# Loading a convolution kernel's input in whole units, issued behind the preceding unit's stores

## The chip, the cores and the metric

The kernel runs on one core of one Trainium2 chip. The metric is the device time of one execution in microseconds (us); lower is better. The core has a matrix engine (PE), a vector engine (DVE), a scalar engine (ACT), a general engine (POOL), and a sync engine (SP) that here does nothing but issue DMA transfers. The transfers run on 16 DMA engines.

## What is computed

`x` is float32 of shape (32, 384, 56, 56). Each image's 384 channels fall into 32 groups of 12. Each group is normalised by its own mean and variance, then each channel is convolved along the height, circularly, with its own 56 taps, a bias is added, and `x` is added back:

```python
x_cat = jnp.concatenate([x, x[:, :, :-1, :]], axis=2)
out = jax.lax.conv_general_dilated(x_cat, weight, window_strides=(1, 1), padding='VALID', dimension_numbers=('NCHW', 'OIHW', 'NCHW'), feature_group_count=x.shape[1])
...
m = jnp.mean(g, axis=(2, 3, 4), keepdims=True)
s = jnp.var(g, axis=(2, 3, 4), keepdims=True)
...
x = x + _L0_conv_ref(_gn(x), L0_conv_weight, L0_conv_bias)
```

## The kernel before, in words

The work is cut into 64 **units** (`UNITS`). A unit is one channel group of 16 images, laid out as 112 partitions (2 images' 56 rows each) by 5376 float32 values, and is kept as two **halves** of 2688 values: half 0 holds channels 0 to 5, half 1 channels 6 to 11. In DRAM the input is padded to 128 partitions, so a half is 1344 KB to load and 1176 KB to store. `xt` has six slots (`XS = 6`), each for one unit; unit n uses slot n % 6. The result is written over the input in the same slot and stored from there, so a slot takes its next load only after its stores have landed. Two units share a set of filter matrices `runs`, which come from `taps` in two transfers of 147 KB each (`load_taps`).

What each engine does for a unit:

- **DVE** runs three units ahead with the statistics: 16 `bn_stats` for unit u + 3 (`stats`, eight on each half) stand between the six evictions of the even channels of unit u (`take`). Before its first instruction on half 0 it waits for that half's load, and before its ninth for half 1. The order in a unit is: 3 chunks, take channel 0, 3 chunks, take 2, 2 chunks, take 4, `add_vars`, 3 chunks (the first of half 1), take 6, `invert`, 2 chunks, take 8, 3 chunks, take 10.
- **POOL** makes small sums of the statistics and the Newton steps for unit u + 2, and adds `x` to the odd channels of unit u (`add_x`), three before the Newton steps and three behind them.
- **ACT** normalises unit u + 1 into `xn` and evicts the odd channels of unit u.
- **PE** does 12 convolutions (`convolve`) for a unit and small matmuls for unit u + 2.

**SP** issues every transfer, in one fixed order and on one queue; an instruction that waits holds all behind it. A half can be stored once DVE's and POOL's last channel of it is done (`store`). For unit u the order is: store half 0 of u; load half 1 of unit u + 5; store half 1 of u; on every odd u the taps of a later group; load half 0 of unit u + 6. Each load waits for the landing of the same half's store from its slot: half 1 of unit u - 1, half 0 of unit u. All six slots are loaded at the start, twelve half loads, with taps and bias between them.

I write S(u,h) for the store and L(n,h) for the load of a half, and L(n) for the load of a whole unit.

Of the kernel before, what the change touches and what calls it, by code (L numbers as in the profile page):

```python
# [13 lines left out]
GROUPS = 32  # L14
# [9 lines left out]
HALVES = 2  # L24
# [5 lines left out]
PER_GROUP = UNITS // GROUPS  # L30
# [6 lines left out]
XS = 6  # L37
# [11 lines left out]
def through(channels, u, c):  # L49

    return u * len(channels) + sum(k <= c for k in channels)


def build(nc, x, taps, bias, out):
    with ExitStack() as ctx:
        def sb(name, shape):
            return ctx.enter_context(nc.sbuf_tensor(name, shape, F32))
# [4 lines left out]
        def sem(name):  # L62
            return ctx.enter_context(nc.semaphore(name))

        xt = sb("xt", [ROWS, XS, HALVES, FREE])
# [23 lines left out]
        p_mean = psum("p_mean", [P, 512])  # L89
        p_var = psum("p_var", [P, 512])  # L90

        x_loaded = [[sem(f"x_loaded{s}_{h}") for h in range(HALVES)] for s in range(XS)]
        out_stored = [[sem(f"out_stored{s}_{h}") for h in range(HALVES)] for s in range(XS)]
        taps_loaded = [sem(f"taps_loaded{s}") for s in range(2)]
        bias_loaded = sem("bias_loaded")
# [19 lines left out]
        def channel_of(tile, slot, c):  # L115
            half = tile[0:P, slot, c // CH, :].rearrange("k (b c w) -> k b c w", b=BP, c=CH)
            return half[:, :, c % CH, :]

        def bias_of(u, c):
            k = u // PER_GROUP * CG + c  # L120
            return bias_all[:, k:k + 1]
# [4 lines left out]
        def bank_bw(c):  # L126
            return bank(c).rearrange("k (b w) -> k b w", b=BP)
# [2 lines left out]

        @block.sync
        def _(sp):
            def load(n, h):
                if n >= UNITS:
                    return
                if n >= XS:
                    sp.wait_ge(out_stored[n % XS][h], 16 * (n // XS))
                sp.dma_start(xt[:, n % XS, h, :], x[n, :, h, :]).then_inc(x_loaded[n % XS][h], 16)

            def load_taps(g):  # L140

                for par in range(PAR):
                    sp.dma_start(runs[par * H:(par + 1) * H, g % 2, par * BLOCK:(par + 1) * BLOCK], taps[g]
                                 ).then_inc(taps_loaded[g % 2], 16)

            def store(u, h):
                last = (h + 1) * CH - 1
                sp.wait_ge(dve_taken, through(DVE_CH, u, last))
                sp.wait_ge(pool_added, through(ACT_CH, u, last))
                sp.dma_start(out[u, :, h, :], xt[0:P, u % XS, h, :]).then_inc(out_stored[u % XS][h], 16)  # L150

            for h in range(HALVES):
                load(0, h)
            for h in range(HALVES):
                load(1, h)
            sp.wait_ge(runs_zeroed, 1)
            load_taps(0)
            sp.dma_start(bias_all[:], bias.broadcast_to([P, C])).then_inc(bias_loaded, 16)
            for n in range(2, XS):
                for h in range(HALVES):  # L160
                    load(n, h)
                if n == 3:
                    load_taps(1)

            for u in range(UNITS):
                store(u, 0)
                if u >= 1:
                    load(u - 1 + XS, 1)
                store(u, 1)
                g = u // PER_GROUP + 2  # L170
                if u % PER_GROUP == PER_GROUP - 1 and g < GROUPS:
                    load_taps(g)
                load(u + XS, 0)
            for s in range(XS):
                for h in range(HALVES):
                    sp.wait_ge(out_stored[s][h], 16 * len(range(s, UNITS, XS)))
# [77 lines left out]
        @block.vector  # L254
        def _(dve):
            nc.vector.memset(eps[:], EPS).then_inc(consts_set, 1)
            nc.vector.memset(runs[:], 0.0).then_inc(runs_zeroed, 1)

            def stats(n, k0, k1):
                for k in range(k0, k1):  # L260
                    h, b = k // BP, k % BP
                    if b == 0:
                        dve.wait_ge(x_loaded[n % XS][h], 16 * (n // XS) + 16)
                    ins = nc.vector.bn_stats(st[:, n % RS, h, b, :], xt[0:P, n % XS, h, b * ROW:(b + 1) * ROW])  # L264
                if k1 == HALVES * BP:
                    ins.then_inc(stats_ready, 1)

            def add_vars(n):
                dve.wait_ge(pvar_ready, n + 1)
                parts = p_var[:, n % RS * SUBS:(n % RS + 1) * SUBS]  # L270
                nc.vector.tensor_reduce(var[:, n % RS, :], parts.rearrange("k (h b e) -> k b h e", h=HALVES, b=BP),  # L271
                                        AXIS.XY, ALU.add).then_inc(var_ready, 1)

            def invert(n):
                dve.wait_ge(std_ready, n + 1)
                nc.vector.reciprocal(r0[:, n % RS, :], std[:, n % RS, :]).then_inc(r0_ready, 1)  # L276

            def take(u, c):
                dve.wait_ge(conv_ready, u * CG + c + 1)
                cell = channel_of(xt, u % XS, c)  # L280
                nc.vector.scalar_tensor_tensor(out=cell, in0=bank_bw(c), scalar=bias_of(u, c), in1=cell,  # L281
                                               op0=ALU.add, op1=ALU.add).then_inc(dve_taken, 1)

            ALL = HALVES * BP
            stats(0, 0, ALL)
            stats(1, 0, ALL // 2)
            add_vars(0)
            stats(1, ALL // 2, ALL * 3 // 4)
            invert(0)
            stats(1, ALL * 3 // 4, ALL)  # L290
            stats(2, 0, ALL // 2)
            add_vars(1)
            stats(2, ALL // 2, ALL * 3 // 4)
            invert(1)
            stats(2, ALL * 3 // 4, ALL)

            dve.wait_ge(bias_loaded, 16)
            ends = (3, 6, 8, 11, 13, 16)
            for u in range(UNITS):
                for k, c in enumerate(DVE_CH):  # L300
                    if u + LEAD_STATS < UNITS:
                        stats(u + LEAD_STATS, ends[k - 1] if k else 0, ends[k])
                    take(u, c)
                    if u + LEAD_COEF < UNITS:
                        if k == 2:
                            add_vars(u + LEAD_COEF)
                        if k == 3:
                            invert(u + LEAD_COEF)
# [138 lines left out]
```

## Time and profile before

| | |
|---|---|
| median of 3 runs (shown) | 880.48 us |
| the profiled execution, its time | 881.76 us |
| its span, first to last instruction | 879.9 us |
| busy: PE, DVE, ACT, POOL | 83%, 77%, 75%, 65% of the span |
| chain that ended last | DMA 52%, PE 13%, POOL 13%, ACT 10%, DVE 8% |
| moved by DMA | 340.64 MB, mean 387 GB/s |
| read and written in DRAM | 185.97 MB, 154.14 MB |
| TensorE clock granted, mean | 0.925 |

The page divides the span into 40 equal slices and gives each engine's busy share in tenths. DMA's row gives the mean over 16 DMA engines. The chain is followed back from the last instruction to whatever released each step. A transfer's time to landing runs from its issue on SP until its last byte is in place, time in the queue behind other transfers included.

### The profile page before, as it was taken

To read this page: it belongs to the slowest core of one execution; us is meant where nothing else is said; L and a number is where in the kernel's file an instruction comes from. 1 tells how busy PE (TensorE), PEld (TensorE's weight loads), DVE (VectorE), ACT (ScalarE), POOL (GpSimd) and SP (SyncE) were. 2 spreads that over 40 slices of the span, in tenths; PEclk is the share of its full clock that TensorE was granted. 3 is DMA by queue.
4 is the path that set the end of the run, shared out by engine and by line. 5 is a ranking of instruction groups with operands and counts; after the bars stand their busy time and mean duration, and the time that the engine had idled before them with its cause. 6 is when DMAs were issued, how large, how long until landed. Compare 5 with 4: busy or idle time off the path is not lost.

```text
span 879.9 us, 8182 instructions
## 1 busy us (share of the span) xinstructions
PE 732.7 (83%) x1920; PEld 513.0 (58%) x1920; DVE 679.5 (77%) x1538; ACT 662.8 (75%) x1026; POOL 571.2 (65%) x1102
## 2 busy tenths in 40 slices
PE   0688898889889888878788887988878988889895
PEld 0456666666566666556565564665655656566664
DVE  7888878897787878778777677877877887788842
ACT  1788788788788878778677776787877867778784
POOL 2467767676676666666675656676766667567665
PEclk9999979998898999899898899899989989899998
DMA  9999999999999999999999999999999999999986
GB/s 355 410 387 399 383 407 396 406 413 410 403 394 374 377 391 389 405 392 388 401 381 396 370 361 386 398 403 398 403 389 387 392 402 400 390 401 409 405 306 229
DMA packets 39472, 340.64 MB, mean 387 GB/s; under 512 B 5008, under 2 KB 5120, under 8 KB 8704
## 3 DMA queue, kind: packets, MB, share of 16 engines
q1 hardware_dynamic: 39424, 340.13, 99.1%
q8 instruction: 15, 0.25, 0.1%
q14 instruction: 33, 0.27, 0.1%
HBM read 185.97 MB, written 154.14 MB: 387 GB/s over the span
## 4 chain that ended last, share of the span: by engine, by line
DMA 52%; PE 13%; POOL 13%; ACT 10%; DVE 8%; issue 3%; SPq 0%; POOLq 0%; ACTq 0%
DMA out<-xt 28%; DMA xt<-x 24%; PE conv L402 12%; POOL xt L235 10%; ACT xn L330 7%; DVE st L264 5%; ACT xn L338 3%; DVE xt L281 2%; PE p_mean L378 1%; POOL newt L227 1%; POOL rstd L228 1%; POOL newt L226 1%; POOL newt L225 1%; POOL shift L229 0%; PE p_var L387 0%
## 5 line engine op out<-in xcount | busy, mean ns | idle before, releaser
L402 PE MATMUL conv<-xn,runs 112*112 112x448 f32 x1536 | 694.5, 602 | 24.6 <-DMA runs<-taps 10.9
L330 ACT ACTIVATE xn<-xt,shift,rstd 112x672 f32<-112x672 f32 x512 | 463.1, 942 | 140.1 <-POOL xt L235 140.1
L402 PEld LDWEIGHTS conv<-xn,runs 112*112 112x112 f32 x1536 | 465.6, 314 | 167.3 <-issue 64.7
L264 DVE BATCH_NORM_STATS2 st<-xt 112x6 f32<-112x336 f32 x1024 | 451.4, 494 | 109.5 <-DMA xt<-x 109.3
L235 POOL TENSOR_TENSOR xt<-xt,xn 112x448 f32<-112x448 f32 x384 | 431.2, 1136 | 81.0 <-ACT xn L338 80.8
L281 DVE SCALAR_TENSOR_TENSOR xt<-conv,bias_all,xt 112x448 f32<-112x448 f32 x384 | 258.5, 673 | 81.1 <-PE conv L402 80.5
L338 ACT ACTIVATE xn<-conv,bias_all 112x448 f32<-112x448 f32 x384 | 235.7, 626 | 47.7 <-PE conv L402 44.9
L378 PE MATMUL p_mean<-msum,neg_mean 112*112 112x8 f32 x128 | 24.5, 263 | 112.2 <-POOL msum L204 112.2
L214 POOL TENSOR_TENSOR dev<-st,nmean 112x16 f32<-112x16 f32 x128 | 24.9, 216 | 134.6 <-ACT nmean L314 134.6
L378 PEld LDWEIGHTS p_mean<-msum,neg_mean 112*112 112x112 f32 x128 | 19.3, 191 | 150.2 <-POOL msum L204 134.4
L386 PEld LDWEIGHTS p_var<-st,avg 112*112 112x112 f32 x128 | 23.6, 210 | 40.6 <-POOL dev L218 25.9
L225 POOL TENSOR_TENSOR newt<-r 112x8 f32<-112x8 f32 x64 | 12.8, 200 | 35.1 <-DVE r L276 32.6
L386 PE MATMUL p_var<-st,avg 112*112 112x32 f32 x128 | 24.9, 281 | 2.1 <-POOL dev L218 2.1
L387 PE MATMUL p_var<-dev,avg_dev 112*112 112x32 f32 x128 | 26.0, 288 | 0.0
L201 POOL TENSOR_TENSOR mpart<-st 112x16 f32<-112x16 f32 x64 | 15.1, 235 | 10.8 <-DVE st L264 10.8
L319 ACT ACTIVATE std<-var,eps 112x8 f32<-112x8 f32 x64 | 18.9, 295 | 4.2 <-DVE var L271 4.2
L314 ACT COPY nmean<-p_mean 112x8 f32<-112x8 f32 x64 | 9.5, 149 | 15.6 <-PE p_mean L378 15.6
L387 PEld LDWEIGHTS p_var<-dev,avg_dev 112*112 112x112 f32 x128 | 20.9, 208 | 0.0
L223 POOL TENSOR_SCALAR hv<-var 112x8 f32<-112x8 f32 x64 | 12.7, 198 | 9.7 <-DVE var L271 4.4
L218 POOL TENSOR_TENSOR dev<-dev 112x32 f32<-112x32 f32 x64 | 15.4, 240 | 5.0
L227 POOL TENSOR_TENSOR newt<-newt,three_halves 112x8 f32<-112x8 f32 x64 | 13.2, 206 | 5.0
L228 POOL TENSOR_TENSOR rstd<-newt,r 112x8 f32<-112x8 f32 x64 | 13.0, 203 | 5.0
(23 smaller groups left out, 69.4 us busy)
## 6 DMA issues: line engine op xcount, KB each, us to landing
xt<-x SPq DMA_DIRECT2D x128, 1344.0 KB, 10.6
out<-xt SPq DMA_DIRECT2D x128, 1176.0 KB, 12.9
runs<-taps SPq DMA_DIRECT2D x64, 147.0 KB
bias_all<-bias SPq DMA_DIRECT2D x1, 168.0 KB, 14.1
```

The costliest lines, as they stand in the source:

```text
L214: ins = nc.gpsimd.tensor_tensor(d[:, h], means, nm, ALU.add)
L227: chained(nc.gpsimd.tensor_tensor(newt[:], newt[:], three_halves[:], ALU.add))
L228: chained(nc.gpsimd.tensor_tensor(rstd[:, r, :], newt[:], r0[:, r, :], ALU.mult))
L235: nc.gpsimd.tensor_tensor(cell, cell, channel_of(xn, u % NS, c), ALU.add).then_inc(pool_added, 1)
L264: ins = nc.vector.bn_stats(st[:, n % RS, h, b, :], xt[0:P, n % XS, h, b * ROW:(b + 1) * ROW])
L281: nc.vector.scalar_tensor_tensor(out=cell, in0=bank_bw(c), scalar=bias_of(u, c), in1=cell, op0=ALU.add, op1=ALU.add).then_inc(dve_taken, 1)
L330: ins = nc.scalar.activation(xn[:, n % NS, :, part], xt[0:P, n % XS, :, part], ACT.Identity, scale=rstd[:, n % RS, b:b + 1], bias=shift[:, ...
L338: nc.scalar.activation(channel_of(xn, u % NS, c), bank_bw(c), ACT.Identity, bias=bias_of(u, c)).then_inc(act_evicted, 1)
L378: nc.tensor.matmul(p_mean[:, n % RS * BP:(n % RS + 1) * BP], neg_mean[:], msum[:, n % RS, :], start=True, stop=True).then_inc(mean_ready, 1)
L386: nc.tensor.matmul(dst, avg[:], squares, start=True, stop=False)
L387: nc.tensor.matmul(dst, avg_dev[:], dev[:, r, :], start=False, stop=True).then_inc(pvar_ready, 1)
L402: nc.tensor.matmul(bank(c), lay[:, :, c], channel_of(xn, u % NS, c), start=True, stop=True).then_inc(conv_ready, 1)
```

## The change

A unit is loaded in one transfer of 128 x 5376 values, with one semaphore per slot. The load waits for both stores from its slot. For unit u SP's order is now: S(u,0), S(u,1), the taps on odd u, L(u + 5), whose slot is that of unit u - 1. DVE waits for a whole unit ahead of its first `bn_stats`. Stores are halves as before, and what the compute engines execute is the same.

```diff
-            def load(n, h):
+            def load(n):
                 if n >= UNITS:
                     return
                 if n >= XS:
-                    sp.wait_ge(out_stored[n % XS][h], 16 * (n // XS))
-                sp.dma_start(xt[:, n % XS, h, :], x[n, :, h, :]).then_inc(x_loaded[n % XS][h], 16)
+                    for h in range(HALVES):
+                        sp.wait_ge(out_stored[n % XS][h], 16 * (n // XS))
+                sp.dma_start(xt[:, n % XS, :, :], x[n]).then_inc(x_loaded[n % XS], 16)
...
             for u in range(UNITS):
-                store(u, 0)
+                for h in range(HALVES):
+                    store(u, h)
+                    g = u // PER_GROUP + 2
+                    if h == 1 and u % PER_GROUP == PER_GROUP - 1 and g < GROUPS:
+                        load_taps(g)
+
                 if u >= 1:
-                    load(u - 1 + XS, 1)
-                store(u, 1)
-                g = u // PER_GROUP + 2
-                if u % PER_GROUP == PER_GROUP - 1 and g < GROUPS:
-                    load_taps(g)
-                load(u + XS, 0)
+                    load(u - 1 + XS)
...
-                    if b == 0:
-                        dve.wait_ge(x_loaded[n % XS][h], 16 * (n // XS) + 16)
+                    if k == 0:
+                        dve.wait_ge(x_loaded[n % XS], 16 * (n // XS) + 16)
```

SP's queue of before, at the first stores of the run (units 0 and 1), with the semaphores that each row waits for; `out_stored0_1` counts stores of half 1 from slot 0:

```order
L150 DMA out<-xt 112x2688 [waits pool_added,dve_taken] x2
L138 DMA xt<-x 128x2688 [waits out_stored0_0]
L150 DMA out<-xt 112x2688 [waits pool_added,dve_taken]
L138 DMA xt<-x 128x2688 [waits out_stored0_1]
L150 DMA out<-xt 112x2688 [waits pool_added,dve_taken]
L143 DMA runs<-taps 56x672 x2
L138 DMA xt<-x 128x2688 [waits out_stored1_0]
```

The same place of the changed kernel, followed by unit 2:

```order
L151 DMA out<-xt 112x2688 [waits pool_added,dve_taken] x4
L144 DMA runs<-taps 56x672 x2
L139 DMA xt<-x 128x5376 [waits out_stored0_1,out_stored0_0]
L151 DMA out<-xt 112x2688 [waits pool_added,dve_taken] x2
L139 DMA xt<-x 128x5376 [waits out_stored1_1,out_stored1_0]
```

Before, L(6,0) stands behind two stores and L(6,1) behind three. Now L(6) stands behind four stores and the taps. Later in the queue every load used to stand between two stores; now two stores stand between two loads.

## Rows read from the trace of the kernel before

**Rows 1.** The page: engines' busy time, and DMA's busy tenths in 40 slices.

```profile
PE 732.7 (83%) x1920; PEld 513.0 (58%) x1920; DVE 679.5 (77%) x1538; ACT 662.8 (75%) x1026; POOL 571.2 (65%) x1102
...
DMA  9999999999999999999999999999999999999986
```

**Rows 2.** Stretches: length, busy of PE, PEld, DVE, ACT, POOL, clock, DMA share, GB/s.

```profile
5.00:12.00 7.00, 0.00 (x0) 0.00 (x0) 5.33 (x13) 0.00 (x0) 0.00 (x0) 1.00 1.01 429
...
300.00:830.00 530.00, 450.31 (x1176) 312.95 (x1176) 412.84 (x941) 403.81 (x626) 348.69 (x667) 0.92 1.01 393
866.00:873.00 7.00, 5.61 (x15) 4.15 (x14) 2.74 (x4) 2.81 (x5) 5.24 (x6) 1.00 0.92 307
```

**Rows 3.** Waits of SP's queue, whole run: total us, times, longest.

```profile
SPq L138 <- DMA out<-xt: 518.0, 115, 7.3
```

**Rows 4.** Waits, 300 to 830 us.

```profile
DVE st L264 <- DMA xt<-x: 103.7, 72, 3.3
```

**Rows 5.** Waits, 90 to 290 us.

```profile
DVE xt L281 <- PE conv L402: 35.6, 36, 2.1
...
DVE st L264 <- DMA xt<-x: 0.2, 1, 0.2
```

**Rows 6.** Chain that ended last, in time: start, us, what; first and last of 15 units.

```profile
91.90 3.27 POOL xt L235 x3
...
271.99 3.27 POOL xt L235 x3
```

**Rows 7.** The same chain later: start, us, what.

```profile
376.93 13.26 DMA out<-xt
390.20 10.29 DMA xt<-x
400.51 1.33 DVE st L264 x3
```

**Rows 8.** The load's line L138, 300 to 830 us: issue to landing.

```profile
DMA to landing us min/median/max: 9.5/10.6/12.3
```

**Rows 9.** The store's line L150, 300 to 830 us: issue to landing.

```profile
DMA to landing us min/median/max: 11.7/13.0/17.3
```

**Rows 10.** Timeline of unit 29: start, us, engine, line, operation [idle before <- releaser].

```profile
407.73 1.33 DVE L264 BATCH_NORM_STATS2 st<-xt 112x6 f32<-112x336 f32 x3 [1.99 <-DMA xt<-x]
...
412.79 0.18 DVE L271 TENSOR_REDUCE var<-p_var 112x8 f32<-112x32 f32 x1
...
414.57 1.33 DVE L264 BATCH_NORM_STATS2 st<-xt 112x6 f32<-112x336 f32 x3 [1.60 <-DMA xt<-x]
...
418.03 3.31 POOL L235 TENSOR_TENSOR xt<-xt,xn 112x448 f32<-112x448 f32 x3
```

**Rows 11.** DVE's timeline at the start: the wait for half 0 of unit 2.

```profile
21.95 3.38 DVE L264 BATCH_NORM_STATS2 st<-xt 112x6 f32<-112x336 f32 x8 [1.72 <-DMA xt<-x]
```

**Rows 12.** SP's timeline, 52 to 59 us: S(1,0), L(6,1), S(1,1), taps.

```profile
52.62 0.32 SPq L150 DMA_DIRECT2D out<-xt  x1
52.99 0.42 SPq L138 DMA_DIRECT2D xt<-x  x1
57.60 0.32 SPq L150 DMA_DIRECT2D out<-xt  x1
57.97 1.08 SPq L143 DMA_DIRECT2D runs<-taps  x2
```

**Rows 13.** Landing of L(6,0) (least) and L(6,1) (most), issued from 49.57 us.

```profile
DMA to landing us min/median/max: 7.8/9.5/11.2
```

**Rows 14.** Landing of the run's first four half loads; the first finds an empty queue.

```profile
DMA to landing us min/median/max: 5.8/10.0/14.4
```

**Rows 15.** DVE's timeline at the end: the last unit's two halves arrive.

```profile
828.11 1.33 DVE L264 BATCH_NORM_STATS2 st<-xt 112x6 f32<-112x336 f32 x3 [1.52 <-DMA xt<-x]
...
834.15 1.33 DVE L264 BATCH_NORM_STATS2 st<-xt 112x6 f32<-112x336 f32 x3 [0.80 <-DMA xt<-x]
```

More of the change, by code:

```diff
@@ L90, in build @@
         p_var = psum("p_var", [P, 512])
-        x_loaded = [[sem(f"x_loaded{s}_{h}") for h in range(HALVES)] for s in range(XS)]
+        x_loaded = [sem(f"x_loaded{s}") for s in range(XS)]
         out_stored = [[sem(f"out_stored{s}_{h}") for h in range(HALVES)] for s in range(XS)]
@@ L150, in store @@
                 sp.dma_start(out[u, :, h, :], xt[0:P, u % XS, h, :]).then_inc(out_stored[u % XS][h], 16)
[L152 to L155, printed above, removed]
+            load(0)
+            load(1)
             sp.wait_ge(runs_zeroed, 1)
@@ L159, in _ @@
             for n in range(2, XS):
-                for h in range(HALVES):
-                    load(n, h)
+                load(n)
                 if n == 3:
```

## The prediction

> **What bounds the kernel now.** I read the page first. PE is the busiest engine at 83%, DVE follows at 77%, but the DMA row stands at 9 from the first slice to the thirty-eighth [rows 1]. By stretches the 16 DMA engines are fully busy (share 1.01) from 300 to 830 us, where they move 393 GB/s [rows 2]. So over most of the run there is no gap that a better order of transfers could fill.
>
> The waits say who follows whom. From 90 to 290 us DVE hardly waits for loads (0.2 us) and waits for PE instead [rows 5]; the chain passes through POOL, ACT and PE, and the fifteen POOL steps from 91.90 to 271.99 us are 14 units apart, 12.86 us a unit [rows 6]. From 300 us on DVE waits 103.7 us in 72 pieces for loads [rows 4]. The chain there is a store's landing (13.26 us), then a load's (10.29 us), then DVE [rows 7]. A unit moves 2 x 1344 + 2 x 1176 + 147 KB = 5.31 MB, which at 393 GB/s is 13.5 us. This is what was measured: L(6,1) was issued at 52.99 and landed 11.2 us later, at 64.2 [rows 12, 13]; L(63,1), the last load, released DVE at 834.15 [rows 15]; the 57 units between took 770 us, 13.51 us each. The six units loaded at the start let compute run at its own 12.86 us for 290 us, and then the supply of data sets the pace.
>
> By the bytes, a half load is 3.5 us of queue, a half store 3.06 us, the taps 0.38 us a unit. The landing times agree: a load has load, store, load to drain (10.1 us; median 10.6 [rows 8]), and a store load, store, load, store (13.1 us; median 13.0 [rows 9]). So a landing time in the middle is queue, with about 0.5 us on top. On an empty queue it is otherwise: the first load took 5.8 us [rows 14], of which its bytes at 429 GB/s [rows 2] are 3.2, so 2.6 us is start and finish.
>
> **The change part by part.**
>
> *SP's wait.* SP sat 518.0 us waiting for stores to land before it could issue loads [rows 3]. In the new order the load waits for stores of the unit before, the later of which was issued a unit (13.5 us) ago and has only what was queued plus 3.1 us ahead. Nearly all of the 518 us goes. It is worth nothing by itself: while SP waited the DMA engines were busy (1.01). Stores now leave when they are computed instead of up to a unit later, and the queue gets shorter by that.
>
> *Does the shorter queue run dry?* One lap spans two units: S(u,1) is issued, L(u+5) behind it lands, DVE starts unit u+2 with it, and S(u+2,1) becomes ready. From DVE's start at 407.73 to the end of POOL's last add at 421.34 is 13.6 us, less the 1.60 us wait at mid-unit [rows 10], 12.0 us. The transfer part is 3.06 + 0.38 + 7.0 + 0.5 = 10.9 us. The lap is 22.9 us plus whatever is still queued when S(u,1) is issued. Two units of DMA work are 27.0 us, so 4.1 us remain queued, more than the 2.6 us of an empty queue's start. On average it stays fed, by 1.5 us. Cost taken 0, and the other end is a rival.
>
> *The start: the first cost.* DVE waited until 21.95 us for half 0 of unit 2 [rows 11]. It now waits for the whole unit, one half load later, 3.2 us at 429 GB/s [rows 2]. `add_vars(1)` stands behind these statistics, ACT's `root(1)` behind that, and the first convolutions behind ACT, so all evictions slip by about 3.3 us. S(1,1) was issued at 57.60 us when compute released it, and is now ready at 60.9. L(6), two half loads that went out at 49.57 and 52.99 us, waits behind it and behind the taps' issue of 1.08 us [rows 12]. All initial loads and S(0,0), S(0,1) have drained by then, so the queue is dry before S(1,0) and again before S(1,1). S(1,1) lands at 60.9 + 2.6 + 3.0 = 66.5 us, and taps and L(6) at 66.5 + 0.4 + 7.0 = 74 us. Before, L(6,1) landed at 64.2. The queue is ten microseconds behind, and since it is the bound from there on, nothing makes them good. The cover that used to exist, the six preloaded units, is spent on this.
>
> *The middle.* 57 units of 13.51 us from 74 us put the landing of L(63) at 844 us, if bytes move as fast as now.
>
> *The end: the second cost.* Before, the last arrival is half 1 of unit 63, at 834.15 us, in the middle of unit 60; half 0 was there at 828.11 [rows 15]. From there to the end of the span are 879.9 - 834.15 = 45.75 us. Now DVE cannot begin unit 60 until the whole unit is in. The part of DVE's unit ahead of half 1 is from 828.11 to 834.15 - 0.80 = 5.2 us, the same as from 407.73 to 412.97 in unit 29 [rows 10]. The tail becomes 51.0 us.
>
> *Sum so far.* 844.1 + 51.0 = 895.1 us of span, 15.2 us more than 879.9.
>
> *Two stores in a row.* The nearest rows for traffic of one kind: loads alone ran at 429 GB/s; in the last stores' stretch, 307 GB/s at a share of 0.92, that is 334 GB/s [rows 2]. Wholly separated, a unit would take 2.41 MB / 334 = 7.2 us for stores and 2.75 / 429 = 6.4 for loads, 14.0 with taps, 0.5 us more than mixed, 28 us in 57 units. The other end: blocks twice as long make no difference, or a long load sheds part of the gap between 393 and 429 GB/s. A block is 6 to 7 us and transfers overlap at its borders, so I take a quarter, +7 us, nearer the mixed row because it is this queue's own.
>
> Span 902 us; the execution's time lies 1.86 us over its span, and the median shown is 1.3 us under the profiled time: 903 us.
>
> A rule that speaks for the change: the Trainium skill (DMA: Bandwidth & Descriptors, "Anatomy of one DMA" and "Bandwidth") gives a transfer from the GpSimd path about 2.0 us fixed plus its bytes at 436 GB/s and advises batches of 1 MiB or more. If each of the 63 merges saved that fixed part, an estimate by that page is 126 us less transfer time. The rows with a full queue, a landing time equal to the sum of the bytes ahead plus 0.5 us, show the fixed part covered by its neighbours.
>
> **The rivals.**
>
> 1. *Same costs at start and end, but the mixed rate holds or improves slightly.* For: loads alone are faster, and a whole load has one start instead of two. Against: the 334 GB/s of stores alone. 895 + 0.6 = 896 us; with 1% less per unit, 888.
> 2. *The queue runs dry in the middle.* The 1.5 us margin is a mean; a slow unit of compute (intervals between POOL's steps reach over 13 us where the clock drops) uses 1 us of it, and the 16 engines need not be in step, so some go idle first. The deciding point is less than 2.6 us queued at S(u,1). At 0.3 to 0.5 us lost a unit on top of the forecast: 920 to 931 us.
> 3. *Faster.* Long loads run at the pure-load rate without stores suffering, until compute's 12.86 us [rows 6] sets the pace: 74 + 57 x 12.86 + 51.0 = 858 us. It needs 0.65 us less per unit, that is 413 GB/s in place of 393 with 44% of the bytes stores. The break-even with 880.5 is 13.25 us a unit. The skill's rule above would act here, and the result would be this, since compute then stops it.
>
> **How the numbers follow.** The forecast (897 to 912 us) gets 0.40, rival 1 (888 to 897) 0.25, rival 2 (over 912) 0.22, rival 3 (under 863) 0.06, and 0.07 lies between 863 and 888. Within 2% of 880.5, about what a measurement tells from no change, ends at 898. So slower 0.60, same 0.34, faster 0.06. The range is 885 to 926: it takes in rival 1 and most of rival 2, and leaves out the full 28 us of separated traffic with a dry queue on top.
>
> **What would show it.** SP's wait for stores nearly gone from its waits. DVE's first wait for unit 2 ending near 25.2 us; L(6) issued near 62 us and landed near 74; DMA below full in the second slice's end and the third (44 to 66 us), about 8 us lost. Then full until about 840. DVE's waits at one place in a unit, not two. A span from L(63)'s arrival to the end of 51 us. GB/s from 300 to 830 of 385 to 393 by the forecast; over 400 would mean rival 3, and a DMA share below 0.97 there rival 2. Wrong at the root would be an L(6) that lands before 68 us, or a tail near 46.

## The result

| | before | changed |
|---|---|---|
| median | 881.64 us (4 runs) | 956.27 us (4 runs, 953.01 to 964.67) |
| ratio | | 1.0909, 95% interval 1.0852 to 1.0966 |
| profiled execution, its time | 881.76 us | 953.01 us |
| its span | 879.9 us | 951.3 us |
| mean DMA rate over the span | 387 GB/s | 358 GB/s |

The change costs 9%. Slower was forecast, at 903 us with a range up to 926; the measured loss is over three times the forecast one, and the range missed it.

Some runs of a kernel come out more than 1.5% above its fastest, and one of the four runs before took 1353.82 us; such runs are left out of the ratios, and of the times given for the experiments below. The two medians of the table alone would give 1.085 in place of the recorded 1.0909, which changes nothing in what follows. An experiment's ratio is to the kernel before, run beside it on the same chip, and experiments are compared with one another by these ratios, since the kernel before itself came out between 873 and 881 us from one set of runs to the next.

### The profile page after: what moved, and what is told of

The parts are those of the page before. It is cut to its first block, busy times and chain, and to the rows that moved or that the text cites. A ratio compares the mean times of both kernels' runs of the same rounds, so it can differ in the third digit from the quotient of the medians.

```text
span 951.3 us, 8176 instructions
## 1 busy us (share of the span) xinstructions
PE 754.4 (79%) x1920; PEld 511.5 (54%) x1920; DVE 669.1 (70%) x1538; ACT 667.6 (70%) x1026; POOL 569.2 (60%) x1102
## 4 chain that ended last, share of the span: by engine, by line
DMA 47%; DVE 22%; POOL 15%; PE 6%; SPq 4%; ACT 2%; issue 2%; POOLq 0%; ACTq 0%
DMA xt<-x 47%; DVE st L262 14%; POOL xt L233 11%; DVE xt L279 7%; PE conv L400 6%; SPq L144 3%; ACT xn L328 2%; SPq L151 1%; ACT xn L336 1%; POOL newt L225 1%; POOL rstd L226 1%; POOL newt L224 1%; POOL newt L223 1%; POOL shift L227 1%; DVE r L274 0%
## 5 line engine op out<-in xcount | busy, mean ns | idle before, releaser
L400 PE MATMUL conv<-xn,runs 112*112 112x448 f32 x1536 | 718.8, 616 | 57.7 <-ACT xn L328 49.0
L400 PEld LDWEIGHTS conv<-xn,runs 112*112 112x112 f32 x1536 | 463.6, 315 | 223.3 <-ACT xn L328 78.1
L199 POOL TENSOR_TENSOR mpart<-st 112x16 f32<-112x16 f32 x64 | 15.0, 234 | 14.7 <-DVE st L262 14.7
## 6 DMA issues: line engine op xcount, KB each, us to landing
xt<-x SPq DMA_DIRECT2D x64, 2688.0 KB, 15.2
```

The costliest lines, as they stand in the source:

```text
L400: nc.tensor.matmul(bank(c), lay[:, :, c], channel_of(xn, u % NS, c), start=True, stop=True).then_inc(conv_ready, 1)
```

## The profile after

The page of the changed kernel, with engines' busy time, DMA's busy tenths and rate in 40 slices, and the transfers (count, KB each, median us to landing):

```profile
PE 754.4 (79%) x1920; PEld 511.5 (54%) x1920; DVE 669.1 (70%) x1538; ACT 667.6 (70%) x1026; POOL 569.2 (60%) x1102
...
DMA  9979999999999999999999999999999999999956
GB/s 363 396 254 377 377 373 383 378 356 363 363 371 364 360 360 377 369 359 365 381 368 372 372 374 375 363 372 371 369 347 370 364 379 378 365 376 363 346 184 223
...
xt<-x SPq DMA_DIRECT2D x64, 2688.0 KB, 15.2
out<-xt SPq DMA_DIRECT2D x128, 1176.0 KB, 9.9
```

Against [rows 1] the DMA row has a dent in the third slice (254 GB/s), at the place where L(6) is late. After that it reads 9 as before, yet the rate is some 370 GB/s where it was 393 [rows 2]. A busy share in tenths hides this. From 100 to 800 us (the five engines, then clock, DMA share, GB/s):

```profile
100.00:800.00 700.00, 574.03 (x1452) 385.08 (x1452) 501.62 (x1160) 504.39 (x778) 430.02 (x825) 0.91 0.98 369
```

What engines waited for, in the whole run (total us, times, longest), first DVE's waits, then SP's:

```profile
DVE st L262 <- DMA xt<-x: 239.2, 62, 6.8
```

```profile
SPq L150 <- POOL xt L233: 680.6, 127, 36.3
SPq L151 <- DVE xt L279: 22.8, 27, 2.3
```

SP's 518 us for stores to land [rows 3] are gone, as forecast. DVE now waits for a load once in a unit, not twice, but 239 us in all, where it was 109 us before. SP waits for POOL, that is for stores to be ready: it is no longer ahead of compute.

The start and the end, in SP's timeline and in DVE's timeline of the changed kernel:

```profile
61.37 0.32 SPq L151 DMA_DIRECT2D out<-xt  x1
61.73 1.67 SPq L144 DMA_DIRECT2D runs<-taps  x2
63.50 2.06 SPq L139 DMA_DIRECT2D xt<-x  x1
```

```profile
25.91 3.38 DVE L262 BATCH_NORM_STATS2 st<-xt 112x6 f32<-112x336 f32 x8 [0.97 <-DMA xt<-x]
...
898.33 1.33 DVE L262 BATCH_NORM_STATS2 st<-xt 112x6 f32<-112x336 f32 x3 [2.88 <-DMA xt<-x]
```

L(6) was issued at 63.50 and released DVE at 76.64; L(63), the last load, released it at 898.33. So the span splits as the forecast did:

| part | before | forecast | changed |
|---|---|---|---|
| arrival of the first refill, L(6,1) or L(6) | 64.2 us | 74 us | 76.6 us |
| 57 units | 13.51 us each | 13.51 + 0.12 us | 14.42 us each |
| from the last arrival to the end | 45.75 us | 51.0 us | 53.0 us |

Start and end cost 12.4 and 7.2 us, the middle 57 x 0.91 = 51.9 us. They make up the 71.4 us between the spans. The middle is what the forecast missed.

The chain of the changed kernel, in time (start, us, what), over one lap of two units:

```profile
88.62 0.32 SPq L151
88.99 1.41 SPq L144
90.44 2.03 SPq L144
92.57 14.36 DMA xt<-x
106.96 1.33 DVE st L262 x3
...
115.60 3.27 POOL xt L233 x3
118.94 0.32 SPq L151
119.30 0.41 SPq L144
119.76 1.24 SPq L144
121.10 12.78 DMA xt<-x
133.90 1.33 DVE st L262 x3
```

L(8) is issued at 92.57 and lands 14.4 us later; DVE to POOL's last add takes 11.9 us; then SP issues the store and the taps, and L(10) at 121.10. This lap returns to the end of the run. Its mean is 2 x 14.42 = 28.8 us. Over the laps from unit 3 to unit 56 that is 12.1 of compute (median 12.0), 2.0 from the last store's issue to the load's, and 14.7 for the load's landing. On odd units, with the taps' issue in between, the last two are 3.5 and 13.3 us, on even units 0.4 and 16.2: nearly the same sum.

A load lands when the last of the 16 engines has done its share. Counted from the landings' records between 100 and 800 us, the first engine is done 11.6 us after the load's issue and the last 14.9 us (medians); the typical distance between them is 3.2 us. By then the engines that were done first have run out of work. Stretches of 2 us around and behind the issue of a load at 525.54 us (columns as above):

```profile
524.00:526.00 2.00, 2.00 (x6) 0.90 (x4) 2.00 (x6) 2.00 (x4) 1.65 (x4) 0.50 0.99 370
526.00:528.00 2.00, 2.00 (x5) 1.20 (x6) 2.00 (x6) 0.91 (x2) 1.14 (x1) 0.50 1.01 296
528.00:530.00 2.00, 2.00 (x4) 0.99 (x3) 1.60 (x6) 1.75 (x4) 1.04 (x1) 0.50 0.96 335
```

The rate falls to 296 GB/s and the share stays at 1.01. The share counts a packet, that is one row's transfer, in the stretch in which it starts, so in stretches this short it can't show a gap. The packets' own records do: from 526 to 528 us 13 of the 16 engines are at work on average. Between 100 and 800 us it is 15.6 of 16, before 15.9; in the two microseconds from 1 us after a load's issue it is 14.7. The gaps belong to the odd units, which have the taps ahead of their load: at the issue of S(u,1) of an odd u 13.6 engines are at work and five to seven microseconds later 13.5, while around S(u,1) of an even u it is never under 15.8.

The packets also take longer. A load's row of 21,504 bytes takes 932 ns on average and a store's row of 10,752 bytes 446 ns, together 457 ns for each 10,752 bytes; before, the rows of loads and stores together took 438 ns. So 1.9% of the lost rate is idle engines and 4.3% is longer packets: about 0.3 and 0.6 us a unit.

## The experiments

Two theories were set against each other. The **lap theory**: a unit's load goes out too late, and the lap shown above holds the pace. The **traffic theory**: two stores in a row, or rows of 21,504 bytes, are slower traffic whatever waits for them. Below, L139 and so on are the load's line in each kernel, and a window row has the DMA share and GB/s last. 5.31 MB divided by that rate is the time of a unit.

**Half loads in the changed order.** The edit is against the kernel before.

```diff
             for u in range(UNITS):
                 store(u, 0)
-                if u >= 1:
-                    load(u - 1 + XS, 1)
                 store(u, 1)
...
-                load(u + XS, 0)
+                if u >= 1:
+                    for h in range(HALVES):
+                        load(u - 1 + XS, h)
```

> The changed order kept (S(u,0), S(u,1), taps, then the load of unit u + 5), but the load goes out as two half loads with a semaphore each, as in the kernel before. Two theories of the changed kernel's 14.4 us a unit. Lap theory: the load is issued too late, and a two-unit lap of landing 14.4 us, compute 12.0 us and issue time sets the pace; half 0 lands some 3.5 us before the whole unit did, so DVE starts earlier, the lap shrinks by up to 3.5 us, and the pace goes back to about 13.5 us a unit: 885 to 900 us. Traffic theory: two stores in a row and loads in blocks twice as long move slower on the 16 engines, whatever is waited for; the blocks are the same here, so 940 to 956 us. If only the 21,504-byte rows are slow: about 905 us with DVE's waits for the first half still there.

911.64 us, ratio 1.0449 (1.0375 to 1.0523). The window from 100 to 800 us:

```profile
100.00:800.00 700.00, 591.33 (x1518) 405.39 (x1517) 528.17 (x1218) 527.16 (x811) 451.89 (x863) 0.91 1.00 385
```

13.8 us a unit, against 14.4. By the ratios the new order alone costs 4.5% and the merge another 4.6%, about 40 us each. The result lies outside what either theory gave, above the lap theory's range, and nearest to the third guess, that the rows of 21,504 bytes alone are slow. That guess is answered in the main by the packets: with seven slots, below, such a row takes 880 ns, twice a half load's row here (444 ns). In the same order a half load changes that row length and when DVE may start.

**The whole load behind the first store.**

```diff
             for u in range(UNITS):
-                for h in range(HALVES):
-                    store(u, h)
-                    g = u // PER_GROUP + 2
-                    if h == 1 and u % PER_GROUP == PER_GROUP - 1 and g < GROUPS:
-                        load_taps(g)
-
+                store(u, 0)
                 if u >= 1:
                     load(u - 1 + XS)
+                store(u, 1)
+                g = u // PER_GROUP + 2
+                if u % PER_GROUP == PER_GROUP - 1 and g < GROUPS:
+                    load_taps(g)
```

> Whole loads, but L(u + 5) is issued behind S(u,0) and ahead of S(u,1), half a unit (about 7 us) earlier. The blocks of one kind in the queue are as long as in the changed kernel: one whole load, then two half stores. Lap theory: the lap loses up to 7 us and DMA alone sets the pace: 13.5 to 13.7 us a unit, 890 to 905 us. Traffic theory: the pace stays at 14.2 to 14.4 us, 940 to 955 us.

978.32 us, ratio 1.1218 (1.1101 to 1.1334): slower than the changed kernel, which neither theory said. The window, what SP waited for and how long a store took to land, from 100 to 800 us:

```profile
100.00:800.00 700.00, 562.63 (x1401) 370.53 (x1401) 481.40 (x1115) 484.28 (x745) 413.90 (x792) 0.91 0.95 353
```

```profile
SPq L138 <- DMA out<-xt: 564.5, 47, 13.7
```

```profile
DMA to landing us min/median/max: 11.9/15.2/17.6
```

Earlier in the order is not earlier in time. L(u+5) waits for S(u-1,1), which was issued just behind L(u+4). Stores land 15.2 us after their issue, those of half 1 14.5 to 14.9 us. That makes a lap of one unit, with at most S(u,0) in the queue when it closes. 5.31 MB at 353 GB/s are 15.0 us, near that landing. My expectation had left out what the moved load waits for.

**The taps behind the load.**

```diff
             for u in range(UNITS):
-                for h in range(HALVES):
-                    store(u, h)
-                    g = u // PER_GROUP + 2
-                    if h == 1 and u % PER_GROUP == PER_GROUP - 1 and g < GROUPS:
-                        load_taps(g)
-
+                store(u, 0)
+                store(u, 1)
                 if u >= 1:
                     load(u - 1 + XS)
+                g = u // PER_GROUP + 2
+                if u % PER_GROUP == PER_GROUP - 1 and g < GROUPS:
+                    load_taps(g)
```

> The changed kernel with the taps issued behind the whole load instead of ahead of it. Lap theory: the taps' two issues on SP took 1.7 to 3.5 us on every second unit ahead of the load; off the lap, 1 to 1.7 us a unit less can be had until DMA binds: 880 to 930 us, likeliest 910. Traffic theory: same bytes, same blocks, 950 to 956 us.

942.1 us, ratio 1.0787 (1.0694 to 1.0879). That is 11 to 14 us less than the changed kernel, under the 26 to 76 us that I expected, and its interval overlaps the changed kernel's, so the gain itself is not clear. The loads' median landing rose from 15.2 to 16.0 us while the issue time ahead of them went down. So most of the 1.7 to 3.5 us that SP spent on the taps was not a delay by itself; time taken from the issue comes back in the queue, as in the odd and even laps of the changed kernel above.

**Seven slots.** `XS = 7` in the changed kernel and in the kernel before.

> The changed kernel with seven slots for units instead of six; everything is waited for one unit earlier relative to its use, so a lap spans three units (39 us for two units' worth of slack before). Lap theory: the lap no longer binds, DMA does, at 13.5 to 13.7 us a unit, and seven preloaded units soften the start: 880 to 900 us. Traffic theory: pace 14.2 us or more: 935 to 950 us.

> The kernel before with seven slots. DMA sets its pace already, so lead is worth nothing in the middle: 13.5 us a unit, 872 to 885 us. Control for the changed kernel with seven slots: if seven slots gave 30 us or more here too, that run would say nothing of the change's lap.

The changed kernel takes 900.93 us, ratio 1.0317 (1.0205 to 1.0429). The kernel before takes 877.7 us, ratio 1.0019 (0.9964 to 1.0073). The changed kernel with seven slots, its window and its transfers:

```profile
100.00:800.00 700.00, 595.97 (x1539) 409.34 (x1538) 530.71 (x1223) 532.94 (x821) 454.10 (x874) 0.91 1.00 388
```

```profile
xt<-x SPq DMA_DIRECT2D x64, 2688.0 KB, 20.9
out<-xt SPq DMA_DIRECT2D x128, 1176.0 KB, 21.8
```

By this rate the changed kernel's unit takes 13.7 us; from the landing of L(7) to that of L(63) it is 13.87 us. By the ratios 5.9%, 52 us, of the loss are gone, with order, blocks and row length unchanged. Of the 46 us between the two profiled spans, 31 lie in the middle. 13 lie at the start, where the seventh preloaded unit covers the late first refill (L(7) lands at 77.9 us in place of 90.9), and 2 at the end. The same slot is worth nothing to the kernel before. Transfers now take 21 us to land and it does no harm, though the first and the last engine of a load are 11 us apart: the queue is deep. This is the strongest evidence for lead. A load's row of 21,504 bytes takes 880 ns here, so most of the slower packets are not a matter of their length either.

**Lead taken from the kernel before.** `XS = 5`, order and half loads as before.

> The kernel before with five slots: a unit of lead is taken from it, order and half loads stay. Lap theory: S(u-1,1) to the landing of L(u+4,1) to S(u+1,1) is 6.8 + 10.6 + 6.8 us = 24.2 us plus backlog, close to the 22.9 us of the changed kernel, so it should run at 14.0 to 14.6 us a unit: 908 to 942 us. If the changed kernel's extra time is not a matter of lead but of whole loads, 880 to 890 us.

913.17 us, ratio 1.0423 (1.0332 to 1.0514), at the near end of the lap theory's range. The window and what SP waited for, from 100 to 800 us:

```profile
100.00:800.00 700.00, 603.42 (x1529) 411.71 (x1528) 537.50 (x1221) 529.17 (x816) 452.00 (x865) 0.89 1.00 386
```

```profile
SPq L149 <- POOL xt L235: 421.6, 101, 7.0
SPq L138 <- DMA out<-xt: 136.9, 81, 4.8
```

SP waits for compute here, as in the changed kernel; with six slots its wait for POOL in this stretch was 4.3 us. But only the time fell into the range. The pace is 13.75 us a unit and not the 14.0 to 14.6 of the lap theory. Of the 31 us between the spans 14 lie at the start (L(6,1) lands at 78.1 us in place of 64.2), 14 in the middle and 3 at the end. Lead matters to this kernel without any merged load, by 0.24 us a unit in the middle.

**Both cures.** The changed order with half loads and seven slots.

> The changed order with half loads and seven slots. The lap is then as long as can be: what is left over the kernel before is the order's cost in traffic plus the late first store-to-load step. By the traffic runs alone 0.2 to 0.35 us a unit: 885 to 900 us. If half loads and seven slots cure different things, the gain over the seven-slot run with whole loads is more than 10 us.

889.5 us, ratio 1.011 (1.0059 to 1.0161), from six of its ten runs; the others took 900 to 922 us. With whole loads and seven slots the ratio was 1.0317 (1.0205 to 1.0429), so half loads still gain 2.1%, 18 us, over it. That is more than the 10 us by which my expectation would tell two cures of different things. Separately half loads win back 4.6% and the slot 5.9%, together 8.0%: they cure in part the same thing and in part not. About the same 1.7% lies between whole and half loads in the transfers alone, below, so the part that lead does not cure may be traffic. That is not shown.

**The transfers alone.** Three kernels contain only SP's part: every transfer of the full kernel, and stores that wait for their own load in place of compute. No statistics, convolution or addition is done. The taps wait in addition for the landing of the set before them in the same place. The edit of the store for the transfers as before:

```diff
-                sp.wait_ge(dve_taken, through(DVE_CH, u, last))
-                sp.wait_ge(pool_added, through(ACT_CH, u, last))
+                sp.wait_ge(x_loaded[u % XS][h], 16 * (u // XS) + 16)
```

> SP's queue of the kernel before alone: the same transfers in the same order, all compute left out, so the output is the padded input's first 112 rows; a store waits only for its own load, a load for its slot's store. The queue is never short of work. Both theories: the pace of the full kernel was DMA's, so 64 units of 13.4 us, less the tail: 850 to 865 us. If compute's own memory traffic slows the DMA engines, it is nearer 800 us (430 GB/s).

> The changed kernel's transfers in their order (whole loads of 21,504-byte rows, two half stores in a row), all compute left out. Traffic theory: blocks of one kind and long rows are slow in themselves: 3 to 5% over the traffic of the kernel before alone, 880 to 905 us. Lap theory: nothing is late here, so within 1.5% of it, the active work of a unit measured with seven slots being 1% over that of before.

> The transfers of the run with half loads in the changed order, all compute left out: tells long rows from long blocks. If blocks cost and rows do not, equal to the changed traffic; if rows cost, equal to the traffic of before; by the lap theory all three are within 1.5%.

> The traffic of the kernel before alone, once more, beside the two changed forms on one chip: 865 to 872 us.

> The changed kernel's traffic alone, again: 891 us as before, 2 to 3% over the traffic of before.

> Half loads in the changed order, alone; the first time 875 and 903 us left it open. If the cost of the changed traffic lies in blocks of one kind, 889 to 893 us, the same as with whole loads; if in the long rows, 865 to 872 us.

| transfers alone | first | again | ratio to the full kernel before, again |
|---|---|---|---|
| as before | 866.8 us | 865.9 us | 0.9881 (0.9758 to 1.0004) |
| as changed | 891.4 us | 890.4 us | 1.0154 (1.003 to 1.0277) |
| changed order, half loads | 875.5 us (the other run 903) | 876.7 us (three runs; the other seven 886 to 917) | 0.9982 (0.9899 to 1.0064) |

The first row shows that the kernel before is bound by its transfers: without any compute they take within 1.5% of its time, a little more than the 850 to 865 us expected. From 100 to 800 us they moved, first as before and then as changed,

```profile
100.00:800.00 700.00, 0.00 (x0) 1.00 1.01 395
```

```profile
100.00:800.00 700.00, 0.00 (x0) 1.00 1.00 389
```

The full kernel before moved 393, so compute hardly slows them. The second row is the traffic theory's part: 24 us over 64 units, 0.37 us a unit, and that with a full queue. Between the landings of L(6) and L(63) in the profiled runs it is 0.31 us a unit (13.42 and 13.73). These 2.8% lie between what the two theories gave, 3 to 5% and under 1.5%. The third row lies between and spreads too far; whether long blocks or long rows cost these 24 us stays open.

**A thin queue without compute.** The changed transfers alone, a unit's stores held until the load four units on has landed.

```diff
-                last = (h + 1) * CH - 1
-                sp.wait_ge(dve_taken, through(DVE_CH, u, last))
-                sp.wait_ge(pool_added, through(ACT_CH, u, last))
+                m = min(u + 4, UNITS - 1)
+                sp.wait_ge(x_loaded[m % XS], 16 * (m // XS) + 16)
```

> The changed kernel's transfers alone, with the stores of unit u held until the load of unit u + 4 has landed, so that the queue runs dry once a unit. If an almost empty queue by itself makes the load's packets slow (932 ns for 21,504 bytes in the changed kernel, 1011 behind the first store, 878 with a full queue), they are over 930 ns here too and a unit takes more than 13.66 + 2.6 = 16.3 us. If it was compute's presence, packets stay near 880 ns and a unit takes about 16 us.

1141.44 us in a single run, 18.1 us a unit:

```profile
100.00:800.00 700.00, 0.00 (x0) 1.00 0.82 294
```

The load's rows took 858 ns, not over 930, and the store's rows 540 ns. The loads' part of this expectation fell: a queue that runs dry does not by itself make the loads' rows slow. But it does make rows slow. Loads and stores together took 481 ns for 10,752 bytes, where the same transfers with a full queue took 439 ns, and no compute ran in either. And compute's presence alone is not the cause, since with seven slots the loads' rows are at 880 ns beside full compute. So longer packets go with a thin queue, in the changed kernel as here. Why, and why once the loads' rows and once the stores', is open.

**Padding and rows.** Two runs on what limits the kernel before. Loads of 112 rows in place of 128:

```diff
-                sp.dma_start(xt[:, n % XS, h, :], x[n, :, h, :]).then_inc(x_loaded[n % XS][h], 16)
+                sp.dma_start(xt[0:P, n % XS, h, :], x[n, 0:P, h, :]).then_inc(x_loaded[n % XS][h], 16)
```

> The kernel before, loading only the 112 rows that are used and not the 16 rows of padding: an eighth of the load bytes less, 4.96 MB a unit in place of 5.31. If bytes on the DMA engines are what bounds the kernel before, a unit takes 12.6 us of DMA, compute's 12.86 us takes over, and the time is about 64 + 57 x 12.86 + 46 = 843 us, 840 to 855. If 7 rows per engine move slower than 8 (the stores' stretch at the end ran at 334 GB/s), the gain is lost: 875 us or more.

926.02 us, ratio 1.0544 (1.0469 to 1.0619), with 7% fewer bytes. And stores of 128 rows in place of 112, the padding dropped on the host:

```diff
-                sp.dma_start(out[u, :, h, :], xt[0:P, u % XS, h, :]).then_inc(out_stored[u % XS][h], 16)
+                sp.dma_start(out[u, :, h, :], xt[:, u % XS, h, :]).then_inc(out_stored[u % XS][h], 16)
```

> The kernel before with stores of 128 rows (the 16 rows of padding written too, and dropped on the host): 2.75 MB a unit stored in place of 2.41. Loads of 112 rows moved at 356 GB/s overall where loads of 128 gave 393, with packets of 482 ns in place of 437. If transfers of 112 rows are slow because of how rows fall to the engines, all packets come near 404 ns: 5.65 MB at up to 430 GB/s, 13.15 to 13.5 us a unit, 862 to 880 us. If bytes alone count, 5.65 MB at 393 GB/s is 14.4 us a unit: 930 us or more.

889.98 us, ratio 1.0103 (1.0048 to 1.0157), with 6% more bytes; this is outside both ranges, nearer to the first. Windows of the two, loads of 112 rows first:

```profile
100.00:800.00 700.00, 584.42 (x1503) 400.99 (x1504) 526.63 (x1201) 519.68 (x802) 443.49 (x853) 0.91 1.01 356
```

```profile
100.00:800.00 700.00, 594.91 (x1563) 411.85 (x1563) 548.19 (x1249) 538.83 (x835) 462.14 (x886) 0.93 1.01 416
```

All-112 traffic moves at 356 GB/s, mixed at 393, all-128 at 416, and DMA is fully busy in each. A row of 10,752 bytes takes 482, 438 and 416 ns on average. The padding of the loads costs nothing; leaving it out does. Padding the stores nearly pays for its own bytes, and no more. No version tried beats the kernel before.

## Why the prediction was right and wrong

- *What bounds the kernel.* Right. Its transfers alone take 867 us.
- *SP's wait for stores.* Right: gone, and worth nothing.
- *The start.* Right in mechanism, 2.4 us too small. L(6) was issued at 63.50 for 62 and landed at 76.6 for 74. Its landing took 13.1 us where I had 11.6 us from my issue at 62.4.
- *The end.* Right in mechanism, 2 us too small: 53.0 us for 51.0.
- *Does the shorter queue run dry?* This step failed. It found a lap of 22.9 us plus the backlog, 4.1 us of backlog at S(u,1), 1.5 us more than an empty queue's start, and took the cost as 0. That made a lap of 27.0 us, 12.0 of compute and 15.0 of transfer. Measured are 28.8 us, 12.1 of compute and 16.7 from the issue of S(u,1) to the landing of L(u+5). The forecast's lap had no issue time, of which 2.0 us stand ahead of the load, and it treated the 16 engines as one. The lap closes when the slowest engine lands the load, 3.2 us behind the fastest, and by then the fastest have run out; 14.7 of 16 are at work after a load's issue. The runs show 0.55 us a unit for this lost lead by arrivals (14.42 us with six slots, 13.87 with seven), 0.7 by the rates. Not all of it is idle engines: packets last longer too, which the forecast had as constant and for which I have no shown cause.
- *Rival 2* was this mechanism and got 0.22. Its condition of engines out of step was right. Slow units of compute are there but count for little: a few laps have up to 14.4 us of compute in place of 12.0, and the mean is 12.1. 0.3 to 0.5 us a unit on top of the forecast's 0.12 was too small, and so the range ended at 926.
- *Two stores in a row.* The forecast took a quarter of 0.48 us, 0.12 us a unit. The transfers alone give 0.31 to 0.37 us, between the middle and the separated end. This term was mis-sized by 11 to 14 us in 57 units. With the 0.55 us of lost lead it makes up about the 0.91 us of the middle.
- *The merge itself* was priced only at the start and the end. In the middle it also costs half a load of lead in each lap, and half loads in the same order win back about 40 us, of the 42 between the profiled spans 36 in the middle.
- *Rival 3 and the Trainium skill's rule.* The Trainium skill (DMA: Bandwidth & Descriptors, "Anatomy of one DMA") counts a fixed part per transfer. Merging 63 pairs, with the order changed too, saved nothing that shows: the transfers alone got 24 us slower, not faster, and with half loads in the changed order they were not slower than with whole ones.
- *What would show it.* The start's signs came true: DVE's wait for unit 2 ended at 25.91 us, and DMA was below full from 44 to 64 us. I named a DMA share under 0.97 for rival 2. The changed kernel's share is 0.98, and its rate 369 GB/s from 100 to 800 us was below the 385 to 393 of the forecast. The rate told it and the share did not.

## What to carry to other kernels

When a kernel is bound by transfers, a new order has to be judged by the lap from a load's issue to the next load that depends on it, and a margin of one or two microseconds in that lap is no margin, since the last of 16 engines closes it (here 3.2 us behind the first) while the first have already run out. Merging two loads saved nothing here while the queue was full, and it makes the consumer wait for the second part before it may use the first. An experiment with one more buffer, and the same buffer in the kernel before as a control, tells lost lead from slow traffic; what it gains at the start has to be taken off first.

## What the runs showed of the hardware

- Transfers of 112 partitions move slower than transfers of 128: 356 GB/s where all are 112, 416 GB/s where all are 128, in rows of 10,752 bytes. Seven rows of 482 ns take about as long as eight of 416 ns.
- A mean busy share of 0.98 to 1.01 went with rates from 356 to 416 GB/s. A busy DMA engine is not one at its peak.
- The 16 engines of one queue are not in step: the first and the last landing of one load's parts are 4.2 us apart in the kernel before, 3.2 us in the changed one, and 11 us in the changed one with seven slots.
- Rows took longer when the queue ran thin, without compute too: 439 ns for 10,752 bytes with a full queue, 481 ns with one that runs dry once a unit.
- In the changed kernel a load behind the taps' issue went out 3.5 us after the store and landed in 13.3 us, one without it 0.4 and 16.2 us: much of what SP spends issuing behind a filled queue is time that the queue would have taken anyway.
